# A decoder layer on one core: the steps of the first two batches in another order on each engine, output weights' split and the third batch's sums inside the attention loop

## The chip, the core and the metric

One core of a Trainium2 chip runs the whole layer in one launch. Its engines are TensorE (PE, with its weight loads as PEld), VectorE (DVE), ScalarE (ACT), GpSimd (POOL) and SyncE (SP), which here only issues DMAs. The metric is the device time in microseconds (us), lower is better.

## The reference, cut to what matters

```python
x = x + attn(layernorm(x), wq, wk, wv, wo)      # 4 batches x 512 tokens x 512, 32 heads of 64, 8 kv heads, RoPE, causal
x = x + cross(layernorm(x), ctx)                # blockwise fp8 rounding of both sides, then x @ ctx^T
x = x + moe(layernorm(x), Wg, W1, W3, W2, sw1, sw3, sw2)   # 8 experts, top 1, capacity 256, and a shared expert
```

All of it is float32 at the interface. The kernel keeps the accuracy of its matmuls by splitting each operand into a high half (`Wh`, `XT[.][:, 0]`, `Oh`, ...) and a rest (`Wl`, `XT[.][:, 1]`, `Ol`, ...); a product is then three matmuls, high by high, high by low, low by high.

## The kernel before, in words

Nothing is planned by a compiler: each engine has its own function with its instructions in a fixed order, and they meet by semaphores that `need.wait_ge` waits on. An engine that waits holds back everything that stands behind the wait on the same engine.

**Attention** (to about 1020 us). There are 32 units (`NU`): two batches by eight key-value groups first (units 0 to 15 alternate between batches 0 and 1), then the same for batches 2 and 3. A unit has four heads, so there are 128 heads (`NH`), and the main loop `for h in range(NH + 7)` runs over them on every engine, each engine with its own lag: PE computes scores of head h, transposes the probabilities of h-2, weighs the values of h-3, and applies the output weights for h-7 (`attn_out`). Between these it projects unit (h+8)//4, three of twelve steps for each head.

**Before the loop** PE runs `first_turn` (the transposes of the normalised x) for the four tiles of batch 0, `project(0, part, c)` for three parts (query halves, then key and value) of twelve matmuls each, `first_turn` for the four tiles of batch 1, `turn_v(0)`, and `project(1, part, c)`. Part 2 of unit 0 uses the PSUM bank of its part 0, so it waits until DVE has rotated that (`rotate(0, 0, fn)`, semaphore `v_ra`). `project(1, ...)` waits for all of batch 1's XT.

Around it, before the change:

- **ACT** (`scalar_engine`): `split_wq(0, .)` (Wh, L874), `first_turn` of batch 0 (XT, L836), `split_wo(0, 0)` and `split_wo(0, 1)` (Oh, L879, which wait for the DMA of the output weights), then for the tiles of batch 2 four `tile_sum` (L848), `tile_means` (L854, L855) and four `tile_squares` (L862), which serve the layernorm of that batch, needed at head 51. Then `values_keys(0)` (kvs, L885), `query_hi(0)` (qh, L906), `first_turn` of batch 1, `value_hi(0)`, four DMAs of `place_queries` (L497), `key_hi(0)` (KT, L900), `split_wq(1, .)`.
- **DVE** (`vector_engine`): statistics (L1199, L1201), reciprocal roots (`rstd_of`, L1180 to L1191) and `first_norm` (L1204) of batch 0, `first_turn` (L1227), `split_wq_lo(0)` (L1235), statistics of batch 1, `split_wo_lo(0)` (L1241, which waits for ACT's split), `rotate(0, 0, .)` (qcs, L1269), `rstd_of` of batch 1, `rotate(0, 1, .)` (q2s, L1269), `first_norm` of batch 1, `key_cos(0)` (kt, L1278), `first_turn` of batch 1, and so on.
- **POOL** (`gpsimd_engine`): `split_wq_lo(0, 0)` and `(0, 2)` (Wl, L1681), `split_wo_lo(0)` (Ol, L1687), `rotate(0)` (L1700, L1701), `query_lo(0)` (ql, L1707), `rotate_key(0)` (L1713, L1716), `key_lo(0)` (L1722), `split_wq_lo(1, 0)`, `rotate(1)`.
- **SP** (`sync_engine`): loads of x, tables and weights, `load_wo(0)` (L1941), `load_wq(1)`, `turn_keys(0)` (krot, L1966, L1967), eight DMAs of `place_queries(.., 0, 0)` which wait for `query_hi(0)`, four more for the low half, then `double_keys(0)` (KT, L1974), for which the first `scores` waits (`d_kt`).

In the loop, heads 0 and 1 follow this chain: `values_keys(1)`, krot by SP, `rotate_key(1)`, at h = 1 `split_wq_lo(1, 2)` on POOL, which waits for ACT's `split_wq(1, 2)` at the top of its h = 1, then `query_lo(1)` and `normalised(0)` (P, L1695), for which PE's `turn_p(0, .)` (L566) waits. DVE's `rotate(2, 0, 0)` at the end of h = 1 waits for `query_lo(1)`. At h = 4 SP issues `turn_keys(2)`, `save_wq(1)` (2 x 768 KB) and `load_background(2)` (xnx, 256 KB), and DVE's `context_max` at the top of h = 5 waits for the last. The sums and squares of batch 3 stand on ACT at h = 0 to 8, those of batch 0 at h = 64 to 72.

Of the kernel before, what the change touches and what calls it, by code (L numbers as in the profile page):

```python
# [125 lines left out]
def decoder(nc, x_in, ctx_in, wqkv_in, wo_in, wg_in, wf_in, ident_in, mask_in, rope_in, ksin_in, rank_in, tri_in, out):  # L126
# [3 lines left out]
    with ExitStack() as root:  # L130
# [697 lines left out]
        def scalar_engine(e):  # L828
# [22 lines left out]
            def tile_means(b):  # L851
                ts, n = slice(b * TB, b * TB + TB), (b - 2) % NB
                need.wait_ge(a_sum, TB * n + TB)
                e.activation(mv[:, ts, 0], ssum[:, 0, ts], ACT.Copy, scale=1.0 / D).then_inc(a_mean, 1)  # L854
                e.activation(ssum[:, 1, ts], ssum[:, 0, ts], ACT.Copy, scale=-1.0 / D).then_inc(a_mean, 1)  # L855
# [20 lines left out]
            def split_wo(ep, half):  # L876
                need.wait_ge(d_wo, 16 * (ep + 1))
                need.wait_ge(p_ao, 8 * ep)
                e.activation(Oh[:, half, :], Oraw[:, half, :], ACT.Copy).then_inc(a_wo, 1)  # L879
# [187 lines left out]
                split_wq(0, part)  # L1067
            for t in range(TB):
                first_turn(t, t)
            split_wo(0, 0)  # L1070
            split_wo(0, 1)
            for t in range(2 * TB, 3 * TB):
                tile_sum(t)
            tile_means(2)
            for t in range(2 * TB, 3 * TB):
                tile_squares(t)
            values_keys(0)
            query_hi(0)
            for t in range(TB, 2 * TB):
                first_turn(t, t - TB)  # L1080
            value_hi(0)
            place_queries(e, need, 0, 1, (0, 1))
            key_hi(0)
            split_wq(1, 0)
            split_wq(1, 1)
            pieces = list(range(NP))
            for h in range(NH + 7):
                unit, k = divmod(h + 8, 4)
                after_unit = 0 < unit <= NU
                if h % 8 == 1 and 0 < h // 8 + 1 <= NSAVE:  # L1090
                    split_wq(h // 8 + 1, 2)
                if h >= 15 and h % 8 == 7 and h // 8 < NEP:
                    split_wo(h // 8, 0)
                    split_wo(h // 8, 1)
                if after_unit and k == 0:
                    values_keys(unit - 1)
                if after_unit and k == 1:
                    value_hi(unit - 1)
                if 0 <= h < NH:
                    exp(h, 3)  # L1100
                    exp(h, 2)
                if 0 <= h - 3 < NH:
                    lower_out(h - 3)
                if h >= SIDE:
                    side_slot(2 * (h - SIDE) - 44)
                if 0 <= h - 2 < NH:
                    pt_hi(h - 2, 0)
                    pt_hi(h - 2, 1)
                    pt_hi(h - 2, 2)
                if after_unit and k == 1:  # L1110
                    key_hi(unit - 1)
                if 0 <= h < NH:
                    exp(h, 1)
                    exp(h, 0)
                if after_unit and k == 0:
                    query_hi(unit - 1)
                if 0 <= h - 3 < NH:
                    pair(h - 3)
                if h % 8 == 5 and 0 < h // 8 + 2 <= NSAVE:
                    split_wq(h // 8 + 2, 0)  # L1120
                if h % 8 == 7 and 0 < h // 8 + 2 <= NSAVE:
                    split_wq(h // 8 + 2, 1)
                for b, at in ((3, 0), (0, 64)):
                    if at <= h < at + TB:
                        tile_sum(b * TB + h - at)
                    elif h == at + TB:
                        tile_means(b)
                    elif at + TB < h <= at + 2 * TB:
                        tile_squares(b * TB + h - at - TB - 1)
                if h - 7 in begins:  # L1130
                    unscaled(begins[h - 7])
                if h - 1 in begins:
                    scaled(begins[h - 1])
                if h + 1 in begins and jobs[begins[h + 1]][0] == "cross":
                    norm_beside(begins[h + 1])
                if 77 <= h < 81:
                    look(h - 77)
                if 52 <= h < 60:
                    first_turn(h - 44, 2)
                if h >= SIDE:  # L1140
                    side_slot(2 * (h - SIDE) - 43)
                for _ in range(pieces_at.get(h, 0)):
                    split_piece(0, pieces.pop(0))
                if h == NH + 1:
                    need.wait_ge(d_k, 48)
                    need.wait_ge(g_const, 1)
                    e.activation(Gh[:, :, 0:8], Graw[:, :, :], ACT.Copy).then_inc(a_const, 1)
                    e.activation(trib[:, :], tri[:, :], ACT.Copy, accum_out=code[:, TB:TB + 1]).then_inc(a_const, 1)
                    e.activation(wam[:, 0, 0:1], wam[:, 0, 0:1], ACT.Silu)
# [16 lines left out]
        def vector_engine(e):  # L1166
# [401 lines left out]
            split_wq_lo(0)  # L1568
            for t in range(TB, 2 * TB):
                first_stats(t)  # L1570
            split_wo_lo(0)
            for fn in range(2):
                rotate(0, 0, fn)
            rstd_of(slice(TB, 2 * TB))
# [13 lines left out]
            for h in range(NH + 7):  # L1588
# [24 lines left out]
                    value_lo(unit - 1)  # L1613
                if unit < NU and k == 2:
                    rotate(unit, 0, 1)
                if h >= 15 and h % 8 == 7 and h // 8 < NEP:
                    split_wo_lo(h // 8)
                if 0 <= h < NH:
# [16 lines left out]
                    rotate(unit, k - 1, 0)  # L1635
                if 0 <= h - 7 < NH:
                    attn_out(h - 7)
                if h == 17:
                    need.wait_ge(a_sq, 2 * TB)
                    need.wait_ge(a_mean, 4)  # L1640
                    rstd_first(slice(2 * TB, 4 * TB), 1.0 / D).then_inc(v_small, 1)
                elif h == 73:
                    need.wait_ge(a_sq, 3 * TB)
                    need.wait_ge(a_mean, 6)
                    rstd_first(slice(0, TB), 1.0 / D).then_inc(v_small, 1)
# [25 lines left out]
        def gpsimd_engine(e):  # L1671
# [168 lines left out]
            e.memset(Zb[:, 0, :], 0.0).then_inc(g_zero, 1)  # L1840
            e.memset(PTh[:, 1152:1280].bitcast(F32), 0.0).then_inc(g_pad, 1)
            e.memset(PTl[:, 1152:1280].bitcast(F32), 0.0).then_inc(g_pad, 1)
            split_wq_lo(0, 0)
            split_wq_lo(0, 2)
            split_wo_lo(0)
            rotate(0)
            query_lo(0)
            rotate_key(0)
            key_lo(0)
            split_wq_lo(1, 0)  # L1850
            rotate(1)
# [1 line left out]
            for h in range(NH + 7):  # L1853
                unit, k = divmod(h + 8, 4)
                after_unit = 0 < unit <= NU
                for part, at in ((0, -10), (2, -7)):
                    ep, rest = divmod(h - at, 8)
                    if rest == 0 and 0 < ep <= NSAVE:
                        split_wq_lo(ep, part)
                if h >= 15 and h % 8 == 7 and h // 8 < NEP:  # L1860
                    split_wo_lo(h // 8)
                if after_unit and k == 1:
# [11 lines left out]
                    pair(h - 3)  # L1874
                if unit < NU and k == 3:
                    rotate(unit)
                for n, at in enumerate((18, 22, 26, 73, 74, 75)):
                    if h == at:
                        newton(slice(2 * TB, 4 * TB) if n < 3 else slice(0, TB), n)
                if h == 76:  # L1880
# [342 lines left out]
```

## Time and profile before

| | us |
|---|---|
| median of 3 runs | 1531.96 |
| lowest, highest of them | 1529.91, 1532.40 |
| the profiled execution, its own time | 1527.53 |
| its span, first to last instruction | 1525.4 |
| PE busy | 1435.0 (94%) |
| DVE, ACT, POOL busy | 1164.8, 973.8, 1030.9 |

The profiled execution took 4.4 us less than the median, and 2.1 us lie outside its span. Busy time of PE is modelled and overlaps; its idle time, and what ended it, is the more reliable reading. Times in the rows count from the first instruction.

### The profile page before, as it was taken

To read this page: it belongs to the slowest core of one execution; us is meant where nothing else is said; L and a number is where in the kernel's file an instruction comes from. 1 tells how busy PE (TensorE), PEld (TensorE's weight loads), DVE (VectorE), ACT (ScalarE), POOL (GpSimd) and SP (SyncE) were. 2 spreads that over 40 slices of the span, in tenths; PEclk is the share of its full clock that TensorE was granted. 3 is DMA by queue.
4 is the path that set the end of the run, shared out by engine and by line. 5 is a ranking of instruction groups with operands and counts; after the bars stand their busy time and mean duration, and the time that the engine had idled before them with its cause. 6 is when DMAs were issued, how large, how long until landed. Compare 5 with 4: busy or idle time off the path is not lost.

```text
span 1525.4 us, 26946 instructions
## 1 busy us (share of the span) xinstructions
PE 1435.0 (94%) x8617; PEld 1264.6 (83%) x8617; DVE 1164.8 (76%) x2810; ACT 973.8 (64%) x2510; POOL 1030.9 (68%) x1057
## 2 busy tenths in 40 slices
PE   5999999999999999799999999888899899999997
PEld 3788888888878888688878878777788888999996
DVE  7688888887888887888888888888576753677773
ACT  4687777777677788578877777765142412555562
POOL 3787898887877889689889978754313131366663
PEclk9999999999999999999999999999999999999999
DMA  6445544334322433324334342603111011587772
GB/s 211 136 111 173 158 111 136 113 86 121 88 84 57 124 101 91 86 78 128 85 94 130 81 123 63 181 10 124 57 41 44 21 43 40 174 264 237 252 245 82
DMA packets 108620, 174.74 MB, mean 115 GB/s; under 512 B 20936, under 2 KB 42696, under 8 KB 108480
## 3 DMA queue, kind: packets, MB, share of 16 engines
q1 hardware_dynamic: 104448, 160.51, 36.3%
q0 software_dynamic: 3840, 12.25, 2.1%
q8 instruction: 70, 1.15, 0.3%
q14 instruction: 70, 0.57, 0.1%
q10 hardware_dynamic: 192, 0.26, 0.1%
HBM read 94.05 MB, written 33.18 MB: 83 GB/s over the span
## 4 chain that ended last, share of the span: by engine, by line
PE 73%; DVE 10%; ACT 9%; issue 4%; DMA 2%; POOL 1%; SPq 1%; DVEq 0%; POOLq 0%; ACTq 0%
PE bank L514 16%; PE bank L516 16%; PE bank L515 16%; PE bank L566 7%; PE bank L532 4%; PE bank L581 4%; PE bank L582 4%; PE bank L533 4%; ACT P L912 3%; DVE PTl L1297 2%; PE bank L506 2%; DVE Zb L1358 1%; ACT Otmp L918 1%; ACT PTh L924 1%; DVE P L1256 1%
## 5 line engine op out<-in xcount | busy, mean ns | idle before, releaser
L912 ACT ACTIVATE P<-P,mn 128x512 f32<-128x512 f32 (+3 forms) x512 | 284.1, 561 | 173.8 <-DVE mn L1256 173.4
L1695 POOL TENSOR_TENSOR P<-P,ri 128x128 f32<-128x128 f32 (+3 forms) x512 | 358.0, 730 | 35.0 <-DVE ri L1245 34.9
L1256 DVE CUSTOM_DVE_ANT_0 P<-bank,mask 128x512 f32<-128x512 f32 (+3 forms) x512 | 228.3, 482 | 84.2 <-PE bank L533 83.2
L1297 DVE TENSOR_TENSOR PTl<-bank,PTh 128x512 fp32r<-128x512 f32 (+1 forms) x384 | 210.0, 595 | 5.2 <-ACT PTh L924 1.3
L924 ACT ACTIVATE PTh<-bank 128x512 fp32r<-128x512 f32 (+1 forms) x384 | 176.1, 528 | 21.7 <-PE bank L566 18.4
L532 PE MATMUL bank<-KT,QT 128*128 128x256 f32 (+2 forms) x512 | 166.1, 334 | 19.9 <-DVE mn L1256 19.9
L514 PE MATMUL bank<-XT,Wh 128*128 128x512 f32 x384 | 163.4, 426 | 8.3 <-DVE XT L1227 3.5
L566 PE MATMUL bank<-ident,P 128*128 128x128 f32 x1280 | 169.3, 276 | 0.2 <-POOL P L1695 0.2
L581 PE MATMUL bank<-PTh,VS 128*128 128x256 f32 (+2 forms) x512 | 161.4, 326 | 8.1 <-issue 3.1
L533 PE MATMUL bank<-KT,QT 128*128 128x256 f32 (+2 forms) x512 | 161.6, 324 | 0.0
L582 PE MATMUL bank<-PTl,VS 128*128 128x256 f32 (+2 forms) x512 | 155.4, 325 | 0.0
L515 PE MATMUL bank<-XT,Wh 128*128 128x512 f32 x384 | 151.8, 395 | 0.0
L516 PE MATMUL bank<-XT,Wl 128*128 128x512 f32 x384 | 151.8, 395 | 0.0
L1733 POOL TENSOR_TENSOR OTl<-Opair,OTh 128x512 fp32r<-128x512 f32 x64 | 86.2, 1348 | 91.1 <-ACT OTh L999 90.8
L566 PEld LDWEIGHTS bank<-ident,P 128*128 128x128 f32 x1280 | 144.5, 142 | 2.5 <-POOL P L1695 0.4
L532 PEld LDWEIGHTS bank<-KT,QT 128*128 128x128 f32 x512 | 96.7, 189 | 35.6 <-DVE mn L1256 24.3
L581 PEld LDWEIGHTS bank<-PTh,VS 128*128 128x128 f32 x512 | 96.8, 189 | 20.5 <-issue 10.2
L514 PE MATMUL bank<-Oh,OTh 128*128 128x512 f32 x256 | 103.8, 405 | 9.3 <-DVE Opair L1291 5.7
L1291 DVE TENSOR_TENSOR Opair<-bank,Otmp 64x512 f32<-64x512 f32 x128 | 87.3, 682 | 32.6 <-ACT Otmp L918 31.0
L1052 ACT ACTIVATE hm<-bank 128x256 f32<-128x256 f32 x96 | 36.3, 378 | 113.0 <-PE bank L516 112.0
L533 PEld LDWEIGHTS bank<-KT,QT 128*128 128x128 f32 x512 | 96.9, 189 | 10.5
L582 PEld LDWEIGHTS bank<-PTl,VS 128*128 128x128 f32 x512 | 96.7, 189 | 10.4
(229 smaller groups left out, 4131.4 us busy)
## 6 DMA issues: line engine op xcount, KB each, us to landing
RW<-in_wf SPq DMA_DIRECT2D x153, 256.0 KB, 3.6
QT<-qh SPq DMA_DIRECT2D x256, 64.0 KB, 2.0
QT<-ql SPq DMA_DIRECT2D x252, 64.0 KB, 2.0
Oraw<-in_wo SPq DMA_DIRECT2D x16, 512.0 KB, 4.7
KT<-KT SPq DMA_DIRECT2D x32, 256.0 KB, 3.1
Wraw<-in_wqkv SPq DMA_DIRECT2D x9, 768.0 KB, 5.1
xnx<-in_ctx SPq DMA_DIRECT2D x24, 256.0 KB, 3.7
saved<-Wh SPq DMA_DIRECT2D x7, 768.0 KB, 3.5
```

Source lines behind the costliest of these rows:

```text
L514: e.matmul(ps, lh, rh, start=start, stop=False)
L515: e.matmul(ps, lh, rl, start=False, stop=False)
L516: return e.matmul(ps, ll, rh, start=False, stop=stop)
L532: e.matmul(ps[:, 0:k], lhs, KT[:, u % 2, 0, 0:k], start=True, stop=False)
L533: e.matmul(ps[:, 0:k], lhs, KT[:, u % 2, 1, 0:k], start=False, stop=True).then_inc(p_s, 1)
L566: last = e.transpose(ps[:, tokens(m)], src, ident[:, :])
L581: e.matmul(ps[:, q:512], lhs, pt_of(PTh, kb), start=kb == 0, stop=False)
L582: last = e.matmul(ps[:, q:512], lhs, pt_of(PTl, kb), start=False, stop=kb == 3)
L912: e.activation(pq, pq, ACT.Exp, bias=mn[:, z, qb:qb + 1], scale=-1.0, accum_out=rs[:, z, qb:qb + 1]).then_inc(a_exp, 1)
L1256: e.tensor_tensor_reduce(P[:, z, off[qb]:off[qb] + k], bank[n % 2][:, 0:k], mask[:, 512 - k:512], -0.125, BIG, ALU.add, ALU.min, mn[:, z, ...
L1297: e.tensor_tensor(pt_part(PTl, part), bank[2 + part][:, 0:128 * n].rearrange("p (m n) -> p m n", n=128), pt_part(PTh, part).bitcast(F32), ...
L1695: e.tensor_tensor(pq, pq, ri[:, z, qb:qb + 1].to_broadcast([128, n]), ALU.mult).then_inc(g_norm, 1)
```

## The change

Nothing is added or removed but one wait; instructions trade places.

- ACT: `split_wo(0, .)`, the sums, means and squares of batch 2 leave the stretch before the loop. `split_wo(0, .)` goes to the top of h = 2; batch 2's sums to h = 0 to 8, batch 3's from there to h = 9 to 17. `query_hi(0)` goes behind `first_turn` of batch 1; `place_queries` of the low half behind `key_hi(0)` and `split_wq(1, 0)`.
- DVE: `split_wo_lo(0)` from ahead of `rotate(0, 0, .)` to the middle of h = 2. The first root step of batches 2 and 3 from h = 17 to 19.
- POOL: a wait for all four `first_norm` of batch 0 (`v_xn`) ahead of `split_wq_lo(0, 0)`. `split_wo_lo(0)` to h = 2, ahead of `normalised(1)` and `key_lo(1)`. `rotate_key(0)` ahead of `query_lo(0)`. Newton steps two heads later.
- PE and SP keep their order.

```diff
@@ ACT, before and in the loop
             for t in range(TB):
                 first_turn(t, t)
-            split_wo(0, 0)
-            split_wo(0, 1)
-            for t in range(2 * TB, 3 * TB):
-                tile_sum(t)
-            tile_means(2)
-            for t in range(2 * TB, 3 * TB):
-                tile_squares(t)
             values_keys(0)
-            query_hi(0)
             for t in range(TB, 2 * TB):
                 first_turn(t, t - TB)
+            query_hi(0)
             value_hi(0)
-            place_queries(e, need, 0, 1, (0, 1))
             key_hi(0)
             split_wq(1, 0)
+            place_queries(e, need, 0, 1, (0, 1))
             split_wq(1, 1)
...
+                if h == 2:
+                    split_wo(0, 0)
+                    split_wo(0, 1)
...
-                for b, at in ((3, 0), (0, 64)):
+                for b, at in ((2, 0), (3, 9), (0, 64)):
@@ DVE
             for t in range(TB, 2 * TB):
                 first_stats(t)
-            split_wo_lo(0)
             for fn in range(2):
                 rotate(0, 0, fn)
...
                     rotate(unit, 0, 1)
+                if h == 2:
+                    split_wo_lo(0)
...
-                if h == 17:
+                if h == 19:
@@ POOL
+            need.wait_ge(v_xn, TB)
             split_wq_lo(0, 0)
             split_wq_lo(0, 2)
-            split_wo_lo(0)
             rotate(0)
+            rotate_key(0)
             query_lo(0)
-            rotate_key(0)
             key_lo(0)
...
+                if h == 2:
+                    split_wo_lo(0)
...
-                for n, at in enumerate((18, 22, 26, 73, 74, 75)):
+                for n, at in enumerate((20, 24, 28, 73, 74, 75)):
```

## Rows read from the trace of the kernel before

**Rows 1.** The chain that ended last, 0 to 90 us: start, length, work.
```profile
7.32 14.25 DMA Oraw<-in_wo
...
38.71 0.43 PE bank L514
...
41.06 0.23 PE bank L514
...
51.95 1.29 POOL Wl L1681
...
71.94 5.70 DMA xnx<-in_ctx
```

**Rows 2.** Busy time by window; x counts instructions, PEclk the granted clock.
```profile
34.00:50.00 16.00, 14.21 (x59) 11.57 (x60) 7.79 (x19) 6.01 (x16) 9.93 (x8) 0.89 0.42 104
...
83.20:90.40 7.20, 7.20 (x43) 6.44 (x42) 6.47 (x19) 7.15 (x22) 5.88 (x7) 1.00 0.20 49
...
126.40:133.60 7.20, 7.20 (x45) 6.22 (x44) 5.52 (x17) 6.09 (x15) 5.93 (x8) 1.00 0.85 302
```

**Rows 3.** Timeline of DVE and POOL, first tiles: start, us, work, idle before.
```profile
9.51 2.67 POOL L1681 TENSOR_TENSOR Wl<-Wraw,Wh 128x512 fp32r<-128x512 f32 x2 [7.95 <-ACT Wh L874]
9.62 2.83 DVE L1204 TENSOR_SCALAR P<-X,mv,rstd 128x512 f32<-128x512 f32 x2
12.38 0.99 DVE L1204 TENSOR_SCALAR P<-X,mv,rstd 128x512 f32<-128x512 f32 x2
```

**Rows 4.** Timeline of PE, turns and first projections of both batches.
```profile
12.51 2.82 PE L506 MATMUL bank<-ident,P 128*128 128x128 f32 x12 [0.30 <-DVE P L1204]
16.84 0.77 PE L514 MATMUL bank<-XT,Wh 128*128 128x512 f32 x1 [1.50 <-DVE XT L1227]
...
21.01 0.39 PE L516 MATMUL bank<-XT,Wl 128*128 128x512 f32 x1
...
25.49 0.47 PE L514 MATMUL bank<-XT,Wh 128*128 128x512 f32 x1 [1.34 <-DVE qcs L1269]
...
35.79 0.47 PE L514 MATMUL bank<-XT,Wh 128*128 128x512 f32 x1 [2.36 <-issue]
...
45.70 0.39 PE L532 MATMUL bank<-KT,QT 128*128 128x512 f32 x1
```

**Rows 5.** Timeline of DVE, 22 to 36 us.
```profile
24.07 1.27 DVE L1269 TENSOR_TENSOR qcs<-bank,rope 128x512 f32<-128x512 f32 x2
...
27.32 1.28 DVE L1269 TENSOR_TENSOR q2s<-bank,rope 128x512 f32<-128x512 f32 x2
28.52 1.95 DVE L1204 TENSOR_SCALAR P<-X,mv,rstd 128x512 f32<-128x512 f32 x2
...
33.20 2.48 DVE L1227 TENSOR_TENSOR XT<-bank,XT 128x512 fp32r<-128x512 f32 x4 [0.28 <-ACT XT L836]
```

**Rows 6.** Timeline of the DMA issues of SP.
```profile
32.71 5.94 SPq L497 DMA_DIRECT2D QT<-qh  x8
38.69 2.49 SPq L497 DMA_DIRECT2D QT<-ql  x4
41.29 0.53 SPq L1974 DMA_DIRECT2D KT<-KT  x1
```

**Rows 7.** DMA issues, 0 to 90 us: KB each, median us to landing.
```profile
KT<-KT SPq DMA_DIRECT2D x3, 256.0 KB, 3.0
```

**Rows 8.** Timeline of ACT, head 0 to head 3.
```profile
51.26 0.61 ACT L874 ACTIVATE Wh<-Wraw 128x512 fp32r<-128x512 f32 x1
...
57.11 0.72 ACT L912 ACTIVATE P<-P,mn 128x512 f32<-128x512 f32 x1 [1.66 <-DVE mn L1256]
```

**Rows 9.** Two lines of DVE over the run: ns min/median/max.
```profile
L1241 DVE TENSOR_TENSOR Ol<-Oraw,Oh x16: 677/708/1372, 22.8 to 1012.6; 128x512 fp32r<-128x512 f32 x16
L1235 DVE TENSOR_TENSOR Wl<-Wraw,Wh x9: 656/1714/1724, 16.6 to 450.9; 128x512 fp32r<-128x512 f32 x9
```

## The prediction, on record before the result was known

> **What bounds the kernel now.** I read the busy shares of the page first: PE is busy 94% of the span, so a change can gain only where PE stands idle, or must delay it. Then the chain that ended last, in order of time. From 82 us to 400 us it is all PE, matmul after matmul, so whatever moves PE at 80 us moves the end by the same amount. Before 80 us it is not PE. The chain goes back to the DMA of the output weights, 14.25 us long, which lands at 21.57 [rows 1]. Nothing needs those weights before head 7; ACT only meets their split ahead of the first two batches' work, and DVE meets its own half ahead of `rotate(0, 0, .)`. Last I read the timelines of the five engines from 0 to 82 us side by side. The reader should see four idle stretches of PE in them: the start to the first projection at 16.84, 1.34 us ahead of part 2 at 25.49, the broken stretch from 28.5 to 35.79, and the wait for xnx from 76.5 to 79.0. [rows 4] hold the first three; the fourth is behind the 5.70 us DMA in [rows 1].
>
> So the sum is that of one question: how much earlier does PE start head 0, and how much of that is left at 80 us.
>
> **First tiles.** The four `first_norm` of batch 0 start at 9.62. The first two take 2.83 us together, beside POOL's two Wl splits of 2.67; the last two take 0.99 [rows 3]. With POOL held back by the new wait, four take 4 x 0.48 = 1.9 us and end at 11.5, and the first ends at 10.1. PE's turns of 12 transposes take 2.82, so a tile takes some 0.85 once it has begun to stream; the second turn begins at 10.2 + 0.85 = 11.05 where it began at 12.51 [rows 4]. ACT's and DVE's part behind it is as before, so the first projection starts at 16.84 - 1.45 = 15.4. POOL's Wl now take 11.5 to 14.2, ahead of that, so the added wait costs nothing; behind it on POOL stand only `rotate(0)` and later work, due at 25 us. Without this cover, that is if the norms stay at 0.95 on the mean, the term is 0.
>
> By the Trainium skill, "GPSIMD Engine Reference", Key points, GpSimd shares its SBUF interfaces with VectorE and contends with VectorE instructions in a 2-port mode or with two SBUF inputs. By that the norms are freed and the term is the 1.45 above; the trace agrees for the norms, and the same sentence speaks against the change further down.
>
> **First products.** The twelve matmuls of `project(0, 0, .)` run from 16.84 to 21.40, eleven steps in 4.17, because the granted clock is at 1.2 GHz until about 20.2: one of 512 columns takes 0.43 at that level and 0.23 at 2.4 GHz, as the two projections of the second stretch show [rows 1, 4]. If the clock rises at the same time of the trace, 1.45 us more at the low rate hold 3.4 matmuls, worth 3.4 x 0.23 = 0.8 us: they end at 20.6. If it rises as long after the first of them as now, they end at 19.95. I take the first and keep 0.65 as the end of the range.
>
> **Batch 1's norms.** DVE then needs qcs 1.27, the root of batch 1 (25.3 to 27.32, 2.0), q2s 1.28, less an overlap of 0.1 at the ends [rows 5]. Today qcs starts at 24.07, held by the weights' DMA. Now it follows the twelfth matmul: 20.7 + 1.25 + 2.05 + 1.2 = 25.2 for the first norm where it was 28.52: -3.3. PE's part 2 finds its bank free at 21.95, before part 1 is through, so the 1.34 us of [rows 4] go. The norms keep their delay by POOL, whose `rotate(0)` still starts right behind q2s; with key_cos they take as long as now, 3.8 us.
>
> **Second projection.** Now ACT has kvs, four XT, and only then `query_hi(0)`. The last norm ends at 29.0; key_cos 29.05 to 29.7; DVE's four XT low halves take 2.48 [rows 5] and end at 32.2. So `project(1, 0, 0)` starts at 32.3 instead of 35.79 [rows 4]: -3.5. It takes 8.25 us at 2.4 GHz (36 x 0.229) and took 9.9 in the trace, where the window 34 to 50 shows a granted clock of 0.89 [rows 2], after PE had stood idle. So its end is at 40.6 to 42.2 instead of 45.7.
>
> **The queries' DMAs, which then decide.** Head 0's scores need `double_keys(0)`, the last of a row of issues on SP that starts when `query_hi(0)` is done. That was 32.71 [rows 6]. Now qh follows the fourth XT on ACT: XT ends at 30.35, qh takes 1.06, so SP starts at 31.4, only 1.3 earlier. SP issues eight and four DMAs in 8.6 us and KT lands 3.0 after its issue [rows 6, 7]: 31.4 + 8.6 + 3.0 = 43.0, later than the projection's end. Before, KT landed at 44.3 and PE came at 45.70, so it was just hidden. PE now starts head 0 at 43.05: **-2.65**. The eight issues took 0.74 each and the four behind them 0.62 [rows 6]; one was held for 1 us while ACT issued its four beside them. Were that not so, head 0 starts at 42.05, -3.65. ACT's own four now stand behind `split_wq(1, 0)`, which waits until 35.3; they land by 42.1 and cost nothing. `rotate_key(0)` ahead of `query_lo(0)` on POOL waits for krot until 29.4 and puts ql at 34.4 and KT's low half at 35.7, both before SP asks for them at 37.4 and 39.9: nothing.
>
> **Heads 0 and 1.** Two chains meet on POOL at 51.87: krot and kt from `values_keys(1)`, and Wh of ACT (51.26 + 0.61 = 51.87 [rows 8]), for which Wl at 51.95 waits [rows 1]. The first moves with the end of the second projection (-3.5 or more), the second with head 0's scores (-2.65). The later one counts, so POOL, `query_lo(1)`, `normalised(0)` and PE's turn of head 0 all move by -2.65. The sums of batch 2 stand where those of batch 3 stood, four sums, means and squares each: no difference to head 8.
>
> **Head 2.** ACT's two Oh take 1.16 us; ACT stood idle 1.66 us there [rows 8]: nothing. If it did not, they would cost 1.16. POOL's Ol, 1.3 us, is ahead of `normalised(1)` and `key_lo(1)`. `normalised(1)` is 3 us early; KT for head 4 lands 1.3 later, 0.7 after PE comes for it, but mask and exp of head 4 stand behind other work of DVE for 2 us: 0 to 0.2. DVE's Ol is the one that costs. It stands ahead of the last two masks of head 2 with 0.96 us of slack behind them. Alone it takes 0.68, which is hidden. But it has two inputs in SBUF, and beside busy POOL the like Wl split takes 1.71 at the median, 0.66 alone [rows 9]; POOL is busy without a break there. Then 1.71 - 0.96 = 0.75 reaches the transposed probabilities, the masks and exps of head 3, kvs of unit 2, and by SP the xnx DMA that PE waits for at 79. The same line L1241 elsewhere took 0.71 at the median and 1.37 at most [rows 9]. I take +0.5, between 0 and 1.1.
>
> By the page named above the two-input form contends with GpSimd; by that alone the term would be the whole 0.75. Its own line's rows say less, hence 0.5.
>
> **Heads 3 to 80 us.** `turn_keys(2)`, `save_wq(1)` and the xnx load keep their order on SP, and the DMA its 5.70 us [rows 1]. The wait at 79 moves with kvs of unit 2; it neither absorbs nor adds.
>
> **Heads 9 to 17.** ACT gets four sums (0.8 each), two small ones and four squares (0.9 each), 7 us in nine heads of 7.2 us. It was busy 6.09 of 7.2 at the fullest there, and PE lost nothing where ACT was busy 7.15 of 7.20, with the same squares at heads 5 to 8 [rows 2]. So 0. The root steps at h = 19 are due at head 51: 0.
>
> **Sum.** -2.65 + 0.5 = -2.15 with the clock rising late and the issue held; each of the two goes the better way about half the time (-0.65, -1.0), and the slower of the paths takes part of it, so I add -0.55: **-2.7 us**. Against the profiled execution: 1527.5 becomes 1524.8. Its own time is 4.4 below the median, so against the median: 1531.96 - 2.7 = 1529.3.
>
> **Rivals.**
> - *Both ends go well:* the clock rises earlier, the issues are not held, DVE's Ol is hidden: -2.65 - 0.65 - 1.0 = -4.3, 1527.7. For it: the 0.62 of the later issues. Against it: ACT's issues still overlap SP's. Chance 0.25.
> - *KT does not bind*, PE goes from the second projection into head 0 at 41: -4.9 + 0.5, 1527.5. It needs 1 us less between qh and KT than any row shows. Chance 0.05.
> - *The change does only part of what it says:* the first norms are slow for another reason than POOL, so the start gains 0 and the norms of batch 1 come 0.8 later, and DVE's Ol costs its full 1.1: -1.85 + 1.1 = -0.8, 1531.2. For it: one case alone shows their delay [rows 3]. Chance 0.2.
> - *Slower:* ACT becomes the bound at heads 9 to 17. It decides once a head's ACT work passes 7.2 us; the fullest window has 6.09 and gets 0.9, so it lacks 0.2. If each of the nine heads then waits 0.8: +7.2 - 2.7 = +4.5, 1536.5. Against it [rows 2]. Chance 0.05.
> - The forecast, 1529.3, has 0.45; its own range is 1528.3 to 1530.5.
>
> **How the numbers follow.** A measurement of this kernel can tell about 0.2%, 3.06 us, from no change; the three runs alone spread over 2.5. The forecast's range crosses that bound: of its 0.45 I count 0.13 as faster. Faster: 0.25 + 0.05 + 0.13 = 0.43. Slower: 0.05 and 0.02 for the spread. Same: 0.5. The range reaches from the two good cases less 0.9 for the spread to the partial case plus 0.4: 1526.8 to 1531.6.
>
> **What would show it.** Right, if the four first norms show 0.5 each, the first projection starts near 15.4, qcs near 20.7, the second projection near 32.3, and PE's idle time ahead of head 0 (none before) is 0.5 to 2.5 us, ended by the KT DMA. DVE's Ol should lie near 55 us with 0.7 to 1.7, and from 82 us on PE should be unbroken, its rows all shifted by the same 2 to 4 us. Wrong, if PE shows gaps at heads 9 to 17 released by ACT's exp or PTh, if the wait for xnx grows, or if head 0 starts at 41.

## The result: 6.6 us slower, and the profile after

The changed kernel took 1539.70 us, the kernel before 1533.08 on the same chip (medians of ten runs each). The ratio is **1.0042**, with an interval of 1.0024 to 1.0061. The forecast was 2.7 us the other way. The new time lies above the range and above the time given for the slower rival. Medians and ratios here are of fast executions; two that fell in the slower state are left out (1599.43 us of `gate_after`, 6812.08 of the kernel before beside it).

| us | before | after |
|---|---|---|
| median of 10 runs | 1533.08 | 1539.70 |
| lowest, highest | 1525.72, 1540.22 | 1535.50, 1547.77 |
| profiled execution, its own time | 1527.53 | 1539.22 |
| its span | 1525.4 | 1537.0 |

The page of the changed kernel, its span, its engines and its chain by engine:

```profile
span 1537.0 us, 26947 instructions
PE 1442.1 (94%) x8617; PEld 1270.9 (83%) x8617; DVE 1169.1 (76%) x2810; ACT 973.9 (63%) x2510; POOL 1030.9 (67%) x1057
PE 73%; DVE 11%; ACT 9%; issue 4%; POOL 1%; DMA 1%; SPq 0%; DVEq 0%; POOLq 0%; ACTq 0%
```

POOL is busy for as long as before, ACT nearly so, and DVE 4.3 us longer, the time that it is held up counted in. PE has the same 8617 matmuls, and 7.1 us more busy time. No engine got more work, so I looked for waits, from the start on.

**The start did what was forecast.** Timelines of DVE and POOL, after (start, us, work, idle before); they answer to [rows 3] and [rows 5]:

```profile
9.54 1.91 DVE L1200 TENSOR_SCALAR P<-X,mv,rstd 128x512 f32<-128x512 f32 x4
11.54 2.50 POOL L1678 TENSOR_TENSOR Wl<-Wraw,Wh 128x512 fp32r<-128x512 f32 x2 [9.99 <-DVE P L1200]
20.82 1.29 DVE L1265 TENSOR_TENSOR qcs<-bank,rope 128x512 f32<-128x512 f32 x2 [1.84 <-PE bank L516]
25.28 1.97 DVE L1200 TENSOR_SCALAR P<-X,mv,rstd 128x512 f32<-128x512 f32 x2
55.82 0.77 DVE L1237 TENSOR_TENSOR Ol<-Oraw,Oh 128x512 fp32r<-128x512 f32 x1
```

PE and SP, after; they answer to [rows 4] and [rows 6]:

```profile
15.33 0.77 PE L514 MATMUL bank<-XT,Wh 128*128 128x512 f32 x1 [1.50 <-DVE XT L1223]
32.20 0.76 PE L514 MATMUL bank<-XT,Wh 128*128 128x512 f32 x1 [1.98 <-issue]
43.36 0.47 PE L532 MATMUL bank<-KT,QT 128*128 128x512 f32 x1 [1.30 <-DMA KT<-KT]
31.47 5.94 SPq L497 DMA_DIRECT2D QT<-qh  x8
```

Four norms take 1.91 us, the first projection starts at 15.33, qcs at 20.82, batch 1's norms at 25.28 and the second projection at 32.20. Head 0 waits 1.30 us for the KT DMA and starts at 43.36, which is 2.3 earlier than in [rows 4].

**The gain is lost after 680 us.** The transposes of the values (L542) come once a unit with the same work around them, so they serve as mileposts. Timeline of PE, before, two of them:

```profile
680.51 0.46 PE L542 MATMUL bank<-ident,kvs 64*128 64x64 f32 x4
...
956.49 0.46 PE L542 MATMUL bank<-ident,kvs 64*128 64x64 f32 x4
```

The same two, after:

```profile
678.08 0.46 PE L542 MATMUL bank<-ident,kvs 64*128 64x64 f32 x4
...
967.81 0.46 PE L542 MATMUL bank<-ident,kvs 64*128 64x64 f32 x4
```

The changed kernel is 2.4 us ahead at 680 us and 11.3 behind at the second of them. By the mileposts between, it stays 2.4 to 3.4 ahead from 97 to 708 us. Then it loses 5.4 between 708 and 743, and 7.7 between 929 and 968 (its own times).

**What stands there.** From head 62 on (498 us) DVE has, beside its masks, background steps of the cross attention's rounding: `steps_of` (L1358, after: L1354) and `large_steps_of` (L1363, after: L1359). Each is a `tensor_scalar` with one input on 128x512 and takes 0.39 us alone. DVE, after, at the first loss:

```profile
711.61 0.17 DVE L1241 RECIPROCAL ri<-rs 128x4 f32<-128x4 f32 x1
711.70 5.53 DVE L1354 TENSOR_SCALAR Zb<-xnx 128x512 uint32<-128x512 uint32 x1
717.14 0.68 DVE L1252 CUSTOM_DVE_ANT_0 P<-bank,mask 128x512 f32<-128x512 f32 x1
```

POOL over the same time, and PE's next scores:

```profile
710.84 1.29 POOL L1713 TENSOR_TENSOR kt<-kt,krot 64x512 f32<-64x512 f32 x1
712.10 1.29 POOL L1730 TENSOR_TENSOR OTl<-Opair,OTh 128x512 fp32r<-128x512 f32 x1
713.35 1.28 POOL L1770 TENSOR_TENSOR xnx<-xnx,Zb 128x512 f32<-128x512 f32 x1
714.60 2.33 POOL L1704 TENSOR_TENSOR ql<-qcs,qh 128x1024 fp32r<-128x1024 f32 x1
716.89 0.58 POOL L1692 TENSOR_TENSOR P<-P,ri 128x128 f32<-128x128 f32 x1
...
717.88 0.58 PE L532 MATMUL bank<-KT,QT 128*128 128x256 f32 x1 [3.43 <-DVE mn L1252]
```

DVE's 0.39 us step takes 5.53. It ends 0.3 us after POOL's `ql` does, so it ran at the boundary between `ql` and `P`, although the records of the two leave no gap; the first `P` takes 0.58 there, and 0.39 where it is alone. So DVE was kept out over four of POOL's instructions, without a gap between them, and got in ahead of the fifth. The mask for which PE waits stands behind it, and PE is idle for 3.43 us. The same step in the kernel before, DVE and POOL:

```profile
714.54 0.39 DVE L1358 TENSOR_SCALAR Zb<-xnx 128x512 uint32<-128x512 uint32 x1
713.15 1.29 POOL L1716 TENSOR_TENSOR kt<-kt,krot 64x512 f32<-64x512 f32 x1
714.59 1.51 POOL L1733 TENSOR_TENSOR OTl<-Opair,OTh 128x512 fp32r<-128x512 f32 x1
```

There DVE came in the 0.15 us between `kt` and `OTl`, and was through at once. The kernel before has such long waits too, at other places (9.89 us at 610, 3.46 at 781, 5.50 at 895). The changed one keeps those three and adds 5.53 at 711 and 6.88 at 933.

The tie that parts them comes one head earlier. In both kernels POOL's `OTl` starts 0.04 us ahead of DVE's step. POOL and DVE, before and then after:

```profile
699.41 1.30 POOL L1733 TENSOR_TENSOR OTl<-Opair,OTh 128x512 fp32r<-128x512 f32 x1 [2.70 <-ACT OTh L999]
699.45 1.54 DVE L1363 TENSOR_SCALAR Zb<-Zb 128x512 f32<-128x512 f32 x1
```

```profile
696.98 1.60 POOL L1730 TENSOR_TENSOR OTl<-Opair,OTh 128x512 fp32r<-128x512 f32 x1 [2.70 <-ACT OTh L999]
697.02 0.40 DVE L1359 TENSOR_SCALAR Zb<-Zb 128x512 f32<-128x512 f32 x1
```

Before (first fence) DVE's step takes 1.54 us and POOL's 1.30: DVE waits. After (second) they take 0.40 and 1.60: POOL waits, by some 0.3. From there the two engines stand otherwise against each other. The other traces agree: wherever the step at this tie took 1.54 (the kernel before and `start_only`), the next one, at about 714, took 0.39 or 0.40, and in the nine others that have DVE's steps in this form and POOL free to run (not the last experiment's) it took 0.39 or 0.40 here and 5.50 to 5.54 there.

**PE's idle time.** Busy time of PE between the two mileposts (columns: window, its length, PE busy, PEclk, DMA share, GB/s), before and then after:

```profile
680.51:956.49 275.98, 266.10 (x1508) 0.99 0.38 101
```

```profile
678.08:967.81 289.73, 271.85 (x1507) 0.97 0.36 96
```

PE stands idle 9.9 us before and 17.9 after, and is busy 5.8 us longer for the same matmuls. The granted clock is 0.99 before and 0.97 after on the mean, and 0.91 in 920 to 960 us after, around the second loss. So of the 13.7 us, 8.0 are idle time, and 5.8 matmuls at the lower level of the clock behind the stops.

The Trainium skill, "SBUF — State Buffer", section "Who interferes with whom", says that GpSimd and VectorE share one pair of ports, that `tensor_scalar` may take it whole in a two-port mode, and that whoever issues first holds it for its instruction while the other is fully blocked. The trace agrees that DVE is blocked and not slowed. But by the page the wait would be one POOL instruction, 1.3 us. Some were of that kind, such as the 1.54 above; this one was the rest of four, 5.53.

### The profile page after: what moved, and what is told of

It reads as the page before. It is cut to its first block, busy times and chain, and to the rows that moved or that the text cites. A ratio compares the mean times of both kernels' runs of the same rounds, so it can differ in the third digit from the quotient of the medians.

```text
span 1537.0 us, 26947 instructions
## 1 busy us (share of the span) xinstructions
PE 1442.1 (94%) x8617; PEld 1270.9 (83%) x8617; DVE 1169.1 (76%) x2810; ACT 973.9 (63%) x2510; POOL 1030.9 (67%) x1057
## 4 chain that ended last, share of the span: by engine, by line
PE 73%; DVE 11%; ACT 9%; issue 4%; POOL 1%; DMA 1%; SPq 0%; DVEq 0%; POOLq 0%; ACTq 0%
PE bank L514 16%; PE bank L516 16%; PE bank L515 16%; PE bank L566 7%; PE bank L532 4%; PE bank L581 4%; PE bank L582 4%; PE bank L533 4%; ACT P L912 3%; PE bank L506 2%; DVE Zb L1354 2%; DVE PTl L1293 2%; DVE P L1252 1%; ACT Otmp L918 1%; ACT PTh L924 1%
## 5 line engine op out<-in xcount | busy, mean ns | idle before, releaser
L1692 POOL TENSOR_TENSOR P<-P,ri 128x128 f32<-128x128 f32 (+3 forms) x512 | 359.6, 734 | 45.4 <-DVE ri L1241 32.1
L532 PE MATMUL bank<-KT,QT 128*128 128x256 f32 (+2 forms) x512 | 167.1, 335 | 28.8 <-DVE mn L1252 26.4
L582 PEld LDWEIGHTS bank<-PTl,VS 128*128 128x128 f32 x512 | 96.6, 189 | 10.4
```

What stands on the lines that cost most here:

```text
L532: e.matmul(ps[:, 0:k], lhs, KT[:, u % 2, 0, 0:k], start=True, stop=False)
L582: last = e.matmul(ps[:, q:512], lhs, pt_of(PTl, kb), start=False, stop=kb == 3)
L1692: e.tensor_tensor(pq, pq, ri[:, z, qb:qb + 1].to_broadcast([128, n]), ALU.mult).then_inc(g_norm, 1)
```

## The experiments

All ratios are to the kernel before, run beside the variant. Its medians there were 1532.54, 1533.25, 1534.72 and 1534.65 us.

**Four theories.** A: DVE's background steps are locked out behind POOL's back-to-back instructions, and that is where PE's time goes. B: the moved sums and root steps cost it. C: what matters is the absolute time at which the loop begins. D: what matters is POOL's own stream, where one more wait ahead of the loop shifts the ties between POOL and DVE.

### Another form of DVE's steps

In the changed form each step has a second input in SBUF, a constant, which `tensor_scalar` hasn't.

```diff
-                e.tensor_scalar(q.bitcast(U32), y.bitcast(U32), 0x7F800000, None, ALU.bitwise_and)...
+                e.tensor_tensor(q.bitcast(U32), y.bitcast(U32), cc[:, 0:1].bitcast(U32).to_broadcast([128, 512]),
+                                ALU.bitwise_and)...
...
-                e.tensor_scalar(q, q, 2.0 ** -6, 1.5 * 2.0 ** 20, ALU.max, ALU.mult)...
+                e.scalar_tensor_tensor(q, q, 2.0 ** -6, cc[:, 1:2].to_broadcast([128, 512]), ALU.max, ALU.mult)...
```

> The kernel before, with the two background steps of DVE (L1358, L1363: mask of the exponent, then max and mult, 20 jobs each) written with a second input in SBUF that is a broadcast constant, instead of the one-input form. Same results. Theory A (the one-input form waits for a whole unbroken run of POOL instructions, up to 9.9 us in the trace, and whether it does is chance of a few tenths of a us): the long waits (9.9, 5.5, 3.5) shrink to the 1.0 us that the two-input form showed at its line for Wl, the time falls by 10 to 20 us to 1513 to 1523, and the spread of the runs falls. Theory B (the moved sums and the moved first steps themselves cost): no change beyond 2 us, both forms wait alike.

Measured: 1539.00 us, ratio 1.0059 (1.0033 to 1.0084).

> The changed kernel with the same two-input form in the 40 background steps. Theory A: 1510 to 1520, and 2 to 3 us BELOW tt_before, since the start gained 3.3 us and only 0.6 went at heads 9 to 17. Theory B: still some 6 us above tt_before.

Measured: 1538.81 us, 1.0041 (1.0024 to 1.0059). The durations of the first step over the run, on the kernel before with this edit (ns min/median/max):

```profile
L1361 DVE TENSOR_TENSOR Zb<-xnx,cc x10: 659/663/5847, 500.3 to 901.5; 128x512 uint32<-128x512 uint32 x10
```

The long waits stayed (four of 4.0 to 5.9 us here, four of 4.1 to 5.9 on the changed kernel), and the steps took 0.66 us alone instead of 0.39. So as a remedy this failed, and both expectations of A with it. It doesn't speak for B either, by which the second would be 6 us above the first; they are 0.2 apart. What it shows is that a form with two SBUF inputs is locked out as well.

### Starting later

The changed kernel with four more statistics on DVE ahead of the norms, which puts the whole loop 2.8 us later.

```diff
                 first_stats(t)
+            for _ in range(4):
+                after()
+                chain(e.bn_stats(st[:, 0, :], X[:, 0, :]))
             rstd_of(slice(0, TB))
```

> The changed kernel with four more statistics of tile 0 on DVE (0.69 us each, 2.8 us in all) ahead of the first norms, so that all of it runs at about the times of the kernel before. Theory A with chance alone: 2.8 us slower than the changed kernel, some 1542, ratio to before 1.006. Theory C (what decides the long waits is where the loop stands against something that runs by absolute time from the launch): back to the kernel before, 1533, ratio 1.000. Theory B: 1542.

Measured: 1541.12 us, 1.0060 (1.0037 to 1.0082). The loop then began about when it did before the change, and the time didn't come back. C falls.

### Each half of the change alone

The start alone: the changed kernel's order ahead of the loop, its wait on POOL and its split of the output weights at head 2. The loop's sums and root steps stay as before, and batch 2's sums on ACT stand ahead of `values_keys(0)`.

```diff
@@ ACT
-            split_wo(0, 0)
-            split_wo(0, 1)
             for t in range(2 * TB, 3 * TB):
                 tile_sum(t)
...
@@ POOL
+            need.wait_ge(v_xn, TB)
             split_wq_lo(0, 0)
```

> The changed kernel, but the sums, means and squares of batch 2 in ACT's idle time of 12 us ahead of the copy of kvs, those of batch 3 back at heads 0 to 8, the root steps back at h = 17, 18, 22, 26: the loop is the kernel before's but for the output weights' split at h = 2. Theory B (sums at heads 9 to 17): 3 to 4 us below before, 1529.5. Theory A: the long waits stay, so anything between 1525 and 1540 with the mean 3 us below before if chance only, or near 1539 if the start's shift brings them.

Measured: 1538.00 us, 1.0039 (1.0020 to 1.0058).

The sums alone: the kernel before, with batch 2's sums at heads 0 to 8, batch 3's at 9 to 17, and the root steps two heads later.

```diff
@@ ACT
-            for t in range(2 * TB, 3 * TB):
-                tile_sum(t)
-            tile_means(2)
-            for t in range(2 * TB, 3 * TB):
-                tile_squares(t)
...
-                for b, at in ((3, 0), (0, 64)):
+                for b, at in ((2, 0), (3, 9), (0, 64)):
```

> The kernel before, and only the sums, means and squares of batch 2 moved from ahead of the loop to heads 0 to 8, those of batch 3 to heads 9 to 17, the root steps to 19, 20, 24, 28; output weights' split and all else as before. Theory B: slower by up to the whole 6.6 us, ratio 1.004. Theory D, with no instruction more on POOL: ratio 1.000 or, with the 6.6 us that ACT saves at the start cut to the wait for the output weights' DMA, some 2 us faster, 0.999.

Measured: 1535.25 us, 1.0009 (0.9997 to 1.0022). B falls: the start carries the loss, though its own timeline is the one that went nearly as forecast.

### One idle wait on POOL

The kernel before, with a wait that is long met when POOL comes to it.

```diff
             e.memset(PTl[:, 1152:1280].bitcast(F32), 0.0).then_inc(g_pad, 1)
+            e.wait_ge(g_pad, 2)
             split_wq_lo(0, 0)
```

> The kernel before with one more wait on POOL ahead of its first Wl split, for a semaphore that POOL itself has just raised: it costs under 0.1 us and moves no work, but every later instruction of POOL stands one place further in its stream, as in the changed kernel. Theory D (ties between DVE and POOL, 0.04 us apart in the traces, fall one way or the other by where the instructions stand in the stream): 1538 to 1540, ratio 1.004. Theory A with plain chance, and the theories that blame the moved work: ratio 1.000.

Measured: 1542.99 us, **1.0071** (1.0054 to 1.0087). It moves no work, and PE starts head 0 at 46.07, 0.4 us from where it did before. One of DVE's steps, over the run:

```profile
L1363 DVE TENSOR_SCALAR Zb<-Zb x20: 392/738/6864, 504.9 to 961.6; 128x512 f32<-128x512 f32 x20
```

Its longest, 6.86 us at 931, is the changed kernel's 6.88 at 933, and it has the wait at 713 too (5.54). Here is the opposite, the changed kernel without the one wait that it added:

```diff
             e.memset(PTl[:, 1152:1280].bitcast(F32), 0.0).then_inc(g_pad, 1)
-
-            need.wait_ge(v_xn, TB)
             split_wq_lo(0, 0)
```

> The changed kernel without its one added wait on POOL (v_xn): the instruction count of POOL is that of the kernel before again, and the first four norms meet POOL's Wl splits as before, which gives back 0.8 to 1.5 us of the start. Theory D (the place of the instructions in POOL's stream decides the ties): 1531 to 1533, ratio 0.998 to 1.000, some 7 us below the changed kernel although its start is slower. Without theory D: 1 us above the changed kernel, 1540.

Measured: 1528.96 us, **0.9974** (0.9950 to 0.9998). Three of the five long waits are left, 6.30, 5.50 and 3.45 us at 612, 713 and 785; the step at 930 took 0.73. PE waited 14.6 us for DVE's masks, where the changed kernel waits 26.4. That is 10.7 us less than the changed kernel by the medians and 10.4 by the two ratios, which were measured apart, although the start got worse without the wait:

```profile
11.87 1.92 DVE L1200 TENSOR_SCALAR P<-X,mv,rstd 128x512 f32<-128x512 f32 x4
17.65 0.77 PE L514 MATMUL bank<-XT,Wh 128*128 128x512 f32 x1 [1.50 <-DVE XT L1223]
```

The first projection starts at 17.65 instead of 15.33, and at the milepost of 97 us 1.7 are left of these 2.3. So the added wait wins some 2 us at the start, and gives back several times that behind 600 us.

### Where the idle wait has to stand

Two of them at the same place; one in the middle of the loop; one behind the loop; and one on DVE.

```diff
@@ POOL, two ahead of the loop
+            e.wait_ge(g_pad, 2)
+            e.wait_ge(g_pad, 2)
             split_wq_lo(0, 0)
@@ POOL, in the loop
+                if h == 40:
+                    e.wait_ge(g_pad, 2)
@@ POOL, behind the loop
+            e.wait_ge(g_pad, 2)
             for s in (-8, -7, -6):
@@ DVE, ahead of the loop
+            e.wait_ge(v_xn, 1)
             split_wq_lo(0)
```

> The kernel before with two idle waits on POOL where pad_before had one (+0.7%). Theory D in its simple form (odd or even place): back to 1533, ratio 1.000. If any shift loses the good ties, or the pattern is longer than two: 1.003 to 1.008 again.

Measured: 1540.08 us, 1.0035 (1.0011 to 1.0060).

> The kernel before with the idle wait of pad_before at head 40 on POOL, in the middle of the attention and ahead of the background work. Theory D: as pad_before, ratio 1.004 to 1.008. If pad_before's loss came from something that its wait shifted at the start: 1.000.

Measured: 1543.07 us, 1.0054 (1.0037 to 1.0071).

> The control to pad_before: the same idle wait on POOL, but behind the attention loop, so that no instruction of the loop stands elsewhere; the stream as a whole is as long as in pad_before. Theory D: ratio 1.000, 1533. If the mere length or layout of the whole program decides: 1.007 as pad_before.

Measured: 1535.48 us, 1.0004 (0.9979 to 1.0030).

> The kernel before with one idle wait on DVE ahead of its first Wl split, for a semaphore long raised. Theory D for POOL's stream alone: 1.000. If any engine of the tie counts: a change of either sign, 0.996 to 1.007.

Measured: 1534.61 us, 1.0005 (0.9993 to 1.0016).

The three with the wait on POOL ahead of the background steps are slower. The one behind the loop and the one on DVE are not. The wait at head 40 leaves the whole start untouched, so no chain from the start is needed. D stands, but not in its form of odd and even places, which two waits should have brought back to 1.000.

The traces, one execution of each kernel, show where it acts. The second step (`large_steps_of`) over the run, of the kernel before, `pad_end` and `pad_mid`:

```profile
L1363 DVE TENSOR_SCALAR Zb<-Zb x20: 398/816/1536, 505.6 to 952.6; 128x512 f32<-128x512 f32 x20
```

```profile
L1363 DVE TENSOR_SCALAR Zb<-Zb x20: 394/800/1539, 508.3 to 951.5; 128x512 f32<-128x512 f32 x20
```

```profile
L1363 DVE TENSOR_SCALAR Zb<-Zb x20: 394/756/6884, 505.5 to 966.4; 128x512 f32<-128x512 f32 x20
```

Its longest is 6.86 to 6.88 us in all six kernels with an added wait on POOL in or ahead of the loop (`after`, `late_after`, `start_only`, `pad_before`, `pad2_before`, `pad_mid`), always at 927 to 940 us, and at most 1.54 in all five without one (`before`, `after_nowait`, `sums_only`, `pad_end`, `pad_dve`). Between the mileposts around it (926 and 956 us in the kernel before) four of the six lose 7.7 us against the kernel before, `start_only` 7.3 and `late_after` 6.4, and the four others without such a wait under 0.1. The wait at about 714, the changed kernel's first loss, is no such mark: `after_nowait`, `sums_only`, `pad_end` and `pad_dve` have it too and lose 5.3 to 5.6 us there, and three of these are as fast as the kernel before by their medians. So the first loss of 5.4 us is most likely one that the kernel before also has in most of its executions, though not in its profiled one, and what the added wait costs is the second. Less the 2.7 us that the changed kernel is ahead from 217 us on, 7.7 leaves 5.0 of the 6.6. Why the ratios of the three differ (0.71, 0.54 and 0.35%) is not explained.

### Taking the ties away

POOL now waits, in its head h ahead of `pair(h - 3)` (OTl), until DVE has done the background step that stands at the top of DVE's head h + 1. So the step mostly runs while POOL stands still.

```diff
+                if h - 2 in begins:
+                    need.wait_ge(v_bm, begins[h - 2] + 1)
+                if h - 3 in begins:
+                    need.wait_ge(v_bq, begins[h - 3] + 1)
                 if 0 <= h - 3 < NH:
```

> The kernel before, with POOL waiting, at heads with background work, for DVE's step of the next head (v_bm, v_bq) ahead of its pair, so that DVE's two-port step never meets a run of POOL instructions longer than one. Theory A (the long waits are DVE locked out by POOL): the waits of 9.9, 5.5 and 3.5 us go, PE's idle time from 600 to 960 us falls by 12 to 16 us, the time to 1518 to 1522, ratio 0.991 to 0.993, if POOL's own idling stays hidden; if that shows, up to 1536. If the waits stay as they are, theory A falls.

Measured: 1515.52 us, **0.9884** (0.9868 to 0.9901): 17.7 us less. The first step, over the run:

```profile
L1358 DVE TENSOR_SCALAR Zb<-xnx x10: 394/714/1252, 498.8 to 881.8; 128x512 uint32<-128x512 uint32 x10
```

None of the forty steps is over 1.3 us, where the longest was 9.9. The wait of PE on DVE's masks (us in total, times, longest), before and then with this wait:

```profile
PE bank L532 <- DVE mn L1256: 19.9, 8, 7.8
```

```profile
PE bank L532 <- DVE mn L1256: 5.5, 4, 2.3
```

And PE's busy time from 560 to 1000 us, before and then with this wait. Of 26.1 us of idle time 16.0 are left, 4.4 of them in one stretch at 952 that is new and not explained:

```profile
560.00:1000.00 440.00, 413.92 (x2336) 0.99 0.38 103
```

```profile
560.00:1000.00 440.00, 424.01 (x2417) 1.00 0.38 104
```

POOL pays with its own idle time: between 500 and 960 us it waits 45.4 us for DVE's steps, most of it at two places:

```profile
POOL qcs L1700 <- DVE Zb L1358: 17.7, 5, 4.7
POOL OTl L1733 <- DVE Zb L1358: 12.5, 10, 2.3
```

PE waits 0.8 us more for POOL (`Ol`) than before. A is shown: without the lock-outs the time goes, in the stretch and by the wait that it names; and it isn't the mere addition of waits to POOL's stream, which made the kernel slower. The other traces agree. PE's wait for the masks is 4.9 to 5.9 us in the three kernels with this wait (profiled executions of 1512.66 to 1516.09 us), 12.9 to 19.9 in three of 1527.53 to 1529.15, and 23.0 to 29.0 in the eight others with the one-input steps, 1532.79 to 1544.96. The same wait on the start alone, and on the whole change:

> The same gate on start_only (the changed start, the loop's sums as before). With the ties taken out of the loop the start's gain must show: 2.5 to 3.5 us below gate_before (theories A and D). If the start itself costs (theory B in its other form), 4 to 6 above gate_before.

Measured: 1512.45 us, 0.9862 (0.9846 to 0.9879).

> The gate of gate_before on the changed kernel as it is. The change is then worth what the trace shows up to 700 us: 3.3 us won at the start, 0.6 to 0.7 lost at heads 9 to 17: 2.7 us below gate_before (1515.5), 1512.8 to 1513.2, and 0 to 0.7 above gate_start (1512.45). If the sums at heads 9 to 17 cost more than the traces show: 1515 or more.

Measured: 1512.44 us over five executions, 0.9857 (0.9826 to 0.9888).

With the ties out, the start of the change is worth 1515.52 - 1512.45 = **3.1 us**; these are four executions of each, and the two sets do not overlap. They spread over 2.6 and 1.5 us, where 17 of the kernel before beside them spread over 8.6. The whole change is worth 3.1 by its median and 4.1 by its ratio, which was measured apart, near the 2.7 expected; its five executions spread over 7.1, so more finely this can't be told.

## Why the prediction was wrong

**First tiles, first products, norms, second projection**: right, each within 0.15 us of the forecast (15.33, 20.82, 25.28, 32.20). The added wait held POOL back as said, and the norms took 0.48 each. The clock did neither of the two things forecast: the matmuls still started 0.43 us apart up to 21.43 us, and 0.23 only from there, where before that came at 20.2. It cost nothing at this place, because the last of the twelve had started at 20.16, but the better case (-0.65) didn't come.

**The queries' DMAs**: right in the path, 0.3 off in size. SP starts at 31.47 for 31.4, head 0 is held 1.30 us by the KT DMA, inside the 0.5 to 2.5, and starts at 43.36 for 43.05: -2.34 instead of -2.65. The 0.3 is the queries' issues, which took 0.2 longer for the four low halves and began 0.1 later. The reason given for the held issue is wrong: one of the eight again took 1.58 us, at 33.29, and ACT issued nothing until 36.69. What holds such an issue is open. The better case (-1.0) didn't come, and the rival in which KT doesn't bind fell.

**Heads 0 to 3**: the terms were mis-sized. DVE's Ol took 0.77 us, near the 0.71 of its own line in [rows 9]. Head 0 is 2.34 us earlier and `kvs` of unit 2, on the path to the xnx DMA, 2.25 (65.84 instead of 68.09), so it cost 0.1 at most where the forecast had 0.5. PE, after, with a wait for the KT of head 4 that it did not have before:

```profile
64.94 0.47 PE L532 MATMUL bank<-KT,QT 128*128 128x512 f32 x1 [1.09 <-DMA KT<-KT]
75.66 0.39 PE L532 MATMUL bank<-KT,QT 128*128 128x256 f32 x1 [0.69 <-DVE mn L1252]
```

PE and SP, before:

```profile
79.02 0.39 PE L532 MATMUL bank<-KT,QT 128*128 128x256 f32 x1 [2.56 <-DVE mn L1256]
69.16 1.61 SPq L1967 DMA_DIRECT2D krot<-kvs  x1
```

The KT wait is longer than the 0.7 forecast, and POOL's Ol ahead of it took 1.74 instead of 1.3. It put PE only 1.5 us ahead at the milepost of 70 us. But PE waits for xnx behind it in any case, so it cost nothing: that wait fell from 2.56 to 0.69. The forecast said that the wait for xnx "neither absorbs nor adds"; it did both. It absorbed the KT wait, and xnx came 3.3 us earlier, not 2.25, for the issue of krot took 0.69 instead of 1.61 us and the DMA 5.51 instead of 5.70.

**ACT at heads 9 to 17**: nearly right. In the fullest window of [rows 2] PE is busy without a break after the change too:

```profile
126.40:133.60 7.20, 7.20 (x43) 6.39 (x43) 5.42 (x16) 6.25 (x17) 5.95 (x5) 1.00 0.65 201
```

PE lost 0.6 us between 155 and 214, where the forecast had 0 and the slower rival 7.2. What took them no wait in the trace shows.

**Sum at 80 us**: -2.7 was forecast, and -3.3 stood there at 97 us and -2.4 at 680. That the first is so near is in part luck. The start gave 0.3 less than its term and neither of the better cases, for which 0.55 was added; Ol cost 0.4 less; and 1.1 came from the krot issue and the DMA, which no term had.

**The step that failed** is the premise ahead of the sum: "From 82 us to 400 us it is all PE, matmul after matmul, so whatever moves PE at 80 us moves the end by the same amount." The chain was read to 400 us of 1525. The waits of PE by releaser would have shown 19.9 us for DVE's masks, in eight waits, the longest 7.8; the two long ones end at 621 and 901 us. A wait of 7.8 us for a mask that takes 0.68 is a collision with something else, and whether it comes can turn on 0.04 us. What stood at 80 us passed nearly whole up to 708 us (2.85 ahead there), and then 13.1 us were lost in two such collisions.

**The price of the added wait**, the other half of that step, was put at nothing ("so the added wait costs nothing"), since nothing was due behind it on POOL. That was right for the start, and wrong by about 10 us for the kernel: 1539.70 with it, 1528.96 without. The collision at 933 us, 7.7 us, is the part of it that shows in each trace with such a wait.

**The rivals** had no case of this kind. The one slower case rested on ACT as the bound at heads 9 to 17, with 5 in 100. The range of 4.8 us for a median was narrower than what single runs of the kernel before spread over, 14.5 us in ten, which the three runs shown hid; they lay within 2.5. And typical runs of before, at 1533, lie 5.6 above its profiled one, about what one more long wait costs, and the wait at 714 that this one lacks is in nine of the ten other traces with the one-input steps and without the last experiment's wait. So even the sum against the profiled execution was made on a run with fewer collisions than most; that it was this is likely, not shown, for only one execution was profiled.

**What stays open.** Why POOL's place in its stream changes who wins a tie of 0.04 us: an idle wait takes no time that a row shows, and in `before` and `pad_before` DVE's first 17 background steps last equally long to 0.04 us, up to the tie at 699. Open too is why DVE is kept out over one of POOL's instructions at one place and over ten at another. How POOL's instructions are fetched or issued would be the next thing to look at; no run here tried it.

## What to carry to other kernels

Ask of a forecast gain not only where it arises but what lies between there and the end: read PE's waits by releaser over the whole span, and where a short instruction sometimes lasts ten times its usual time, count a shift upstream as a new throw of the dice and widen the range by what one such wait costs. Where DVE has a step beside POOL's work ahead of a mask that PE needs, let POOL wait for that step; here that took 1.2% off. Compare variants of the start only with such ties taken out, or their differences of 3 us drown in those of 5 to 10. And lay the traces of all variants side by side, step by step: what parts two traces need not be what parts their medians, as the wait at 714 shows.

## What the runs showed of the hardware

- **A row of POOL instructions without a gap can lock DVE out over several of them**, not over one alone: waits of 3.5, 5.5, 6.9 and 9.9 us for a step of 0.39, the last over the rest of ten instructions in a row. Others end after one (1.54 at 699). DVE also gets in where the records leave no gap, and then POOL's next instruction takes 0.2 us longer (0.58 instead of 0.39 at 716.89). A gap of 0.15 us between two of them let DVE in at once.
- **The two-input form doesn't escape it**: 5.93 us at most (`tt_after`), 0.66 alone.
- **One wait more in POOL's stream, met long before, changed the kernel by +0.7%** (two of them by +0.35%, one in the middle of the loop by +0.54%), and the one taken out of the changed kernel by -0.7%. The like on DVE or behind the loop did nothing that can be measured.
